# Loops written out on every engine after the first attention, and a constant moved from SBUF to a PSUM column

## The reference, cut to what matters

```
x = x + tanh(g_xattn[0]) * attention0(layernorm(x), ctx)            # 16 heads, softmax
x = x + tanh(g_ffn[0])   * bitnet(layernorm(x))                     # quantised 256->1024, conv of 3 taps, silu, quantised 1024->256
x = x + tanh(g_xattn[1]) * attention1(layernorm(x), ctx, Wq, Wk, Wv) # projections with relu, 16 heads
x = x + tanh(g_ffn[1])   * experts(layernorm(x))                    # 8 experts of width 128, the 2 best of 2 groups
```

## Time and profile before

| | us |
|---|---|
| median of 3 runs | 1893.88 |
| lowest and highest of them | 1891.81, 1896.88 |
| the profiled execution | 1889.21 |
| its span, first to last instruction | 1887.5 |

### The profile page before, as it was taken

The page is one execution under the profiler, slowest core; times in us unless marked ns, Lnnn a source line. Parts: engine busy times, 40 slices in busy tenths (PEclk is TensorE's granted clock), DMA queues, the critical chain, the costliest instruction groups (busy, mean ns, idle before and its releaser), DMA issues. The chain is left out here.

```text
span 1887.5 us, 52415 instructions
## 1 busy us (share of the span) xinstructions
PE 1598.1 (85%) x20058; PEld 1093.4 (58%) x20058; DVE 1574.0 (83%) x2977; ACT 1186.2 (63%) x1916; POOL 865.3 (46%) x932
## 2 busy tenths in 40 slices
PE   0799999846766676748999999996899999999998
PEld 0677777623444444435777777775465565655655
DVE  7799999858888889876888888886888888888885
ACT  1799989778777787716888888886233333323332
POOL 1455555427777777753333333332233333333332
PEclk9999999979999989969999999998899999999999
DMA  9200000000000000000002000000221211222212
GB/s 313 89 3 3 3 3 3 3 0 1 1 0 0 0 0 0 0 17 2 3 2 69 2 2 2 2 2 2 68 91 57 101 67 56 100 67 70 98 57 68
DMA packets 45470, 67.43 MB, mean 36 GB/s; under 512 B 6272, under 2 KB 36736, under 8 KB 45312
## 3 DMA queue, kind: packets, MB, share of 16 engines
q1 hardware_dynamic: 42944, 65.03, 10.4%
q10 hardware_dynamic: 2368, 0.02, 0.1%
HBM read 56.39 MB, written 8.65 MB: 34 GB/s over the span
## 5 line engine op out<-in xcount | busy, mean ns | idle before, releaser
L716 ACT ACTIVATE a_exp<-a_score_t 128x1024 f32<-128x1024 f32 x256 | 262.4, 1025 | 82.5 <-PE a_score_t L526 81.8
L641 DVE TENSOR_REDUCE a_maxes<-a_score 128x8 f32<-128x1024 f32 x256 | 311.0, 1215 | 0.5 <-PE a_score L509 0.5
L1539 POOL TENSOR_TENSOR e_a_parts<-e_act,e_a_parts 128x512 f16<-128x512 f32 x128 | 153.3, 1198 | 332.5 <-ACT e_a_parts L1510 332.5
L1510 ACT ACTIVATE e_a_parts<-e_act 128x512 f16<-128x512 f32 x128 | 80.6, 630 | 314.1 <-DVE e_act L1342 309.2
L1087 POOL TENSOR_TENSOR b_hidden<-b_hidden,b_shifted 128x508 f32<-128x508 f32 x128 | 161.7, 1263 | 124.4 <-DVE b_hidden L937 124.1
L1224 PE MATMUL e_up_ps<-e_n_turned,e_up_t 128*128 128x512 f16 x768 | 187.9, 381 | 9.7 <-DVE e_act L1338 9.7
L1238 PE MATMUL e_out<-e_down_t,e_a_parts 128*128 128x256 f16 x1536 | 188.5, 273 | 0.8 <-POOL e_a_parts L1539 0.8
L1224 PE MATMUL e_gate<-e_n_turned,e_gate_t 128*128 128x512 f16 x768 | 187.9, 381 | 0.2 <-issue 0.2
L1238 PEld LDWEIGHTS e_out<-e_down_t,e_a_parts 128*128 128x128 f16 x1536 | 149.6, 98 | 39.1 <-POOL e_a_parts L1539 1.1
L1094 POOL TENSOR_TENSOR b_hidden<-b_hidden,b_scales 128x512 f32<-128x512 f32 x128 | 168.2, 1318 | 2.9 <-ACT b_scales L1069 2.9
L774 POOL TENSOR_TENSOR a_split<-ctx,a_split 128x256 f16<-128x256 f16 (+1 forms) x64 | 42.9, 671 | 268.6 <-ACT a_split L733 268.6
(11 more groups left out here) (206 smaller groups left out, 4041.7 us busy)
## 6 DMA issues: line engine op xcount, KB each, us to landing
ctx<-e_weights SPq DMA_DIRECT2D x64, 512.0 KB, 5.7
out<-x SPq DMA_DIRECT2D x16, 512.0 KB, 2.9
x<-in_x SPq DMA_DIRECT2D x3, 2048.0 KB, 19.0
ctx<-in_ctx SPq DMA_DIRECT2D x1, 4096.0 KB, 27.0
ctx<-in_ctx SPq DMA_DIRECT2D x1, 3072.0 KB, 16.5
a_exp<-in_L_ffn_w SPq DMA_DIRECT2D x2, 1024.0 KB, 9.7
x<-in_x SPq DMA_DIRECT2D x1, 1536.0 KB, 16.4
ctx<-in_ctx SPq DMA_DIRECT2D x1, 1024.0 KB, 13.4
```

What stands on the lines that cost most here:

```text
L641: nc.vector.tensor_reduce(maxes[:, p * PAIRS:(p + 1) * PAIRS], score[:, :].rearrange("p (h k) -> p h k", k=P), AX.X, ALU.max).then_inc(max ...
L716: nc.scalar.activation(exp32[:, u % 2, 2 * p:2 * p + 2, :], score_t[:, :].rearrange("p (g n) -> p g n", g=2), ACT.Exp, scale=DH ** -0.5 / ...
L1539: nc.gpsimd.tensor_tensor(a_parts[:, e % 4, 1, :], act3[:, e % 2, :], a_parts[:, e % 4, 0, :], ALU.subtract).then_inc(alo_ok, 1)
```

## The change

`run_steps` becomes `write_steps` for VectorE, ScalarE and GpSimd in the second attention, for all four compute engines in the bitnet stage, and for these four and SyncE in the expert stage. The first attention keeps its loops. The SBUF column `level` is dropped; 1/127 goes to column 1 of the PSUM bank `magic`, and L962 and L973 read it there.

```
 # attention_stage, in each of VectorE, ScalarE, GpSimd
-                run_steps(dve, step, UNROLL, head, TILES, last_lag)
+                if layer:
+                    write_steps(step, UNROLL, TILES, last_lag)
+                else:
+                    run_steps(dve, step, UNROLL, head, TILES, last_lag)
...
 # bitnet_stage
-        level = sb("level", [P, 1])
...
-                run_steps(pe, step, 2, head, GROUPS, lag)
+                write_steps(step, 2, GROUPS, lag)
...
-                nc.vector.memset(level[:], 1.0 / 127.0).then_inc(level_ok, 1)
+                nc.vector.memset(magic[:, 1:2], 1.0 / 127.0).then_inc(level_ok, 1)
...
-                    nc.vector.scalar_tensor_tensor(out=peak_mid[:], in0=peak_mid[:], scalar=1e-5, in1=level[:, 0:1].broadcast_to([P, GT]),
+                    nc.vector.scalar_tensor_tensor(out=peak_mid[:], in0=peak_mid[:], scalar=1e-5, in1=magic[:, 1:2].broadcast_to([P, GT]),
...
-                    nc.vector.scalar_tensor_tensor(out=peak_in[:], in0=peak_in[:], scalar=1e-5, in1=level[:, 0:1].broadcast_to([P, GT]),
+                    nc.vector.scalar_tensor_tensor(out=peak_in[:], in0=peak_in[:], scalar=1e-5, in1=magic[:, 1:2].broadcast_to([P, GT]),
...
 # expert_stage, in each of SyncE, TensorE, VectorE, ScalarE, GpSimd
-                run_steps(pe, step, 2, head, GROUPS, lag, first=2)
+                write_steps(step, 2, GROUPS, lag, first=2)
```

More of the change, by code:

```diff
@@ L764, in step @@
                                              scale=gate[:, 0:1]).then_inc(v_ok, 1)
-                run_steps(act, step, UNROLL, head, TILES, last_lag)
+                if layer:
+                    write_steps(step, UNROLL, TILES, last_lag)
+                else:
+                    run_steps(act, step, UNROLL, head, TILES, last_lag)
             @block.gpsimd
@@ L796, in step @@
                         nc.gpsimd.tensor_tensor(m.x[:, t, :], m.x[:, t, :], mixed[:, (u - FL) % 2, :], ALU.add).then_inc(fin_ok, 1)
-                run_steps(pool, step, UNROLL, head, TILES, last_lag)
+                if layer:
+                    write_steps(step, UNROLL, TILES, last_lag)
+                else:
+                    run_steps(pool, step, UNROLL, head, TILES, last_lag)
 def bitnet_stage(nc, io, m):
@@ L1018, in step @@
                                                     x_turned[:, u % 2, d, 0, :, :], ALU.subtract).then_inc(lo_ok, 1)
-                run_steps(dve, step, 2, head, GROUPS, lag)
+                write_steps(step, 2, GROUPS, lag)
             @block.scalar
@@ L1074, in step @@
                                                  ACT.Copy).then_inc(hi_ok, 1)
-                run_steps(act, step, 2, head, GROUPS, lag)
+                write_steps(step, 2, GROUPS, lag)
             @block.gpsimd
@@ L1094, in step @@
                             nc.gpsimd.tensor_tensor(h, h, scales[:, (u - back) % 2, :], ALU.mult).then_inc(mult_ok, 1)
-                run_steps(pool, step, 2, head, GROUPS, lag)
+                write_steps(step, 2, GROUPS, lag)
 def load_experts(nc, sp, io, m):
@@ L1212, in step @@
                         spread_weights(s - 1, u - 1)
-                run_steps(sp, step, 2, head, GROUPS, lag, first=2)
+                write_steps(step, 2, GROUPS, lag, first=2)
                 sp.wait_ge(stored, 16 * GROUPS)
@@ L1463, in step @@
                             norm(s)
-                run_steps(dve, step, 2, head, GROUPS, lag, first=2)
+                write_steps(step, 2, GROUPS, lag, first=2)
             @block.scalar
@@ L1514, in step @@
                             split(s)
-                run_steps(act, step, 2, head, GROUPS, lag, first=2)
+                write_steps(step, 2, GROUPS, lag, first=2)
             @block.gpsimd
@@ L1542, in step @@
                             split_low(s)
-                run_steps(pool, step, 2, head, GROUPS, lag, first=2)
+                write_steps(step, 2, GROUPS, lag, first=2)
 def build_program(nc, io):
```

## The result

The changed kernel takes 1878.66 us in the median of 4 runs (1877.62 to 1879.04), beside 1894.95 us for the kernel before on the same chip. The ratio is 0.9915, with a 95% interval from 0.9898 to 0.9932: 16.1 us, 0.85% faster. The forecast was 1881.6 us, with a range from 1872 to 1891. The profiled execution took 1878.45 us, 10.8 less than that of before; its span is 1876.7 us. By the traces the 10.8 are 5.3 us in the bitnet stage, 4.4 in the experts and 1.2 in the first attention. The code of the first attention is unchanged, and over the runs that keep its loops its length varies by 2.3 us (310.0 to 312.3, from the first to the last L641), so the 1.2 is no part of the change.

A forecast was written before the change was run, and what follows sets the result against it. PE was taken to bound the second attention and nearly the experts, a multi-engine chain the bitnet stage. Terms 0 + 4.3 + 0 + 1.0 + 6.2 + 0.8 = 12.3 us gave a median of 1881.6 us, range 1872 to 1891.

The forecast's parts named there:

- What bounds the kernel: Per stage: PE in the second attention and nearly so in the experts; a chain through several engines in the bitnet stage.
- Second attention, SP's stream: Writing out the second attention's loops, and SP's stream in the experts, was costed at 0 us each.
- Experts: Expert stage loops written out: 0.36 us less in each of 12 steps, 4.3 us in all.
- a second, smaller hold: PE at the turning of the experts' routing weights: the rest of the 0.36 us a step beyond the up product.
- The constant: L962 in the bitnet stage no longer held by POOL: 0.48 us in 13 steps, 6.2 us, plus 0.8 at pipeline's end.
- The bitnet loops: Bitnet stage loops written out: 0.17 us for each pair of steps, 1.0 us in all.
- The sum against the profiled execution: Whole kernel: terms summing to 12.3 us, taken from the profiled 1889.2 us, give 1876.9 us.
- From there to the median: Whole kernel: the profiled execution lay 4.7 us below the median of 1893.88 us, so the median forecast was 1881.6 us.
- The constant's gain: Rival, bitnet chunk 3: waiting for ACT takes back what L962 wins, leaving 5.3 us from loops, 1888.6 us; chance 0.14.
- waited for instructions: Rival, written-out stages: engines stand still for 20 to 30 more instruction packets, about 20 us, 1902 us; chance 0.08.
- Returning: Rival, all loops: each return fetches its code again, so 21 us more are won, 1861 us; chance 0.04.
- The clock's drops: Rival, bitnet steps: without three slow steps 1876.5 us, chance 0.08; with four more slow steps 1888.4 us, chance 0.06.

The follow-up runs named there:

- the extra matmuls: PE repeats the coming chunk's product, unused, before both input turnings of each bitnet step; added to the changed kernel 1871.84 us, to the kernel before 1883.88 us.

## Why the prediction was right, point by point

**What bounds the kernel.** Right for each stage: the second attention gave nothing, the experts what PE could win, the bitnet stage what its chain could win. The parts measured alone are 0 + 4.0 + 6.0 + 6.1 = 16.1 us, and so is the whole; each part is uncertain by some 2 us, and the two edits of the bitnet stage share some of their gain, so the exact agreement is chance.

**Second attention, SP's stream.** Costed at 0; no change in the stage's 427.0 us, nor in the time.

**Experts.** Forecast 4.3, measured 4.0 us, and 4.5 in the stage of the profile. The step is the 34.10 us of the written one. What the prediction called a second, smaller hold, the turning of the routing weights, is the larger: 0.27 us of a step, against 0.11 at the up product.

**The constant.** The mechanism was right: the hold goes, the gain stops at ACT's tap, and DVE waits 0.51 us there. Forecast 6.2 + 0.8 = 7.0; measured 6.1 with the loops kept, and 5.6 after the loops, where a step gains 26.09 - 25.69 = 0.40 us and not 0.48, and the step in which the loop began gains nothing. The two edits of this stage share 0.09 us a step.

**The bitnet loops.** This term was mis-sized: "Written out I give each pair 0.17 us" took the shorter of the two steps for one without a loop's cost. It has 0.09 us of its own. The chain's part is 2.6 us by the stage once the clock's falls cost nothing: about 0.16 in each of 11 steps and 0.85 in the one that misses the hold. The times of the same two kernels say 3.4. The Trainium skill, "Advanced Engine Details and Errata", Control Flow Timing, whose branch gave an estimate of 0.65, is lower than all of these; by that figure, 0.11 of the 0.34 us that a pair gains would be the branch. What the remaining 2.6 to 3.4 of the 6.0 us are isn't shown: the 6.0 alone are uncertain by 2.3 us. The clock may have them: a slow step costs 1.46 to 1.70 us in that kernel and 1.46 to 1.79 in the kernel before, and their number differs between executions of one code. Counted by the starts of chunk 0, the three profiled executions with the bitnet code of before (that of before, of the second attention's loops alone and of the experts' loops alone) have 3, 6 and 5 slow steps; that of the bitnet loops alone has 4.

**The sum against the profiled execution.** The forecast was 1876.9, and the profiled execution of after took 1878.45. In the bitnet stage 8.0 us were forecast. The stage with the extra matmuls shows 404.1 - 395.9 = 8.2, the chain without the clock. In the two profiled executions it shows 409.0 - 403.7 = 5.3, since after has five slow steps and before only three. That 8.2 meets 8.0 is luck: the constant came out 1.4 us lower than forecast and the loops 1.6 higher. With the extra matmuls in both kernels, whole profiled executions differ by 1882.16 - 1870.41 = 11.75 us, against the 12.3 of the sum.

**From there to the median.** The step that subtracted 12.3 from the median of 1893.88 took the clock's bill to be the same in both kernels. Measured were 16.1 us, 12.9 at least by the interval, so 12.3 lies just under it. The profiled execution of before, with three slow steps, was 5.7 us under its median of 1894.95; that of after is 0.2 under its own. With extra matmuls in both kernels the ratios are 0.9961 and 0.9893: 0.0068 x 1891 = 12.9 us. The other 3 us would be the clock, which by these ratios costs before 7.4 us and after 4.2; by the medians after pays 6.8, by the stage in the profiles 7.8. The comparisons have an uncertainty of the same size, so how the last 3 us divide stays open.

**The rivals.** The constant's gain wasn't taken back. No engine waited for instructions: the Trainium skill, "Runtime: NRT & Kernel Launch", Instruction fetch mechanics, says that straight code is streamed with its cost mostly hidden, and 56 more packets without idle time agree. Returning wasn't dear either: all loops together gave 9.1 us, not the 21 and more of that rival. The clock's drops met the shorter steps elsewhere, at 20 us instead of mostly at 16 to 17; in the profiles they cost five steps 6.9 us, against 4.9 us for three before. Neither of the two forecasts for them came true.

## What to carry to other kernels

Look for a tiny instruction that lasts as long as its neighbour on GpSimd, and give it an operand in PSUM; count what that wins only up to the next wait on the same engine. Before writing a loop out, see which engine sets that stage's pace, and check afterwards whether an instruction now starts together with one on another engine that makes it longer: here that cost 22 us. Where a step's length jumps without a change in its work, look at the granted clock, at the place in the step where it falls, and at what waits for TensorE there.

## What the runs showed that was not expected

- A one-tensor `tensor_scalar` of 128x4 elements is held for 1.18 us by a GpSimd instruction, like the two-tensor form; with a PSUM column 0.16 us.
- With GpSimd's start at 0.01 instead of 0.11 us behind VectorE's, VectorE's 128x256 normalisation takes 0.84 instead of 0.40 us in the mean of the tiles, and the kernel is 22 us slower.
- Eight useless matmuls a step made the kernel 6.8 us faster by the medians (4.2 by the ratios, 7.8 in the profiles' bitnet stage). The granted clock still fell to the 1.2 GHz level, but at another place of the step, where the next step did not become late by it.
- Writing the loops out moved one of the held instructions out of its neighbour's way: in one step it took 0.25 instead of 1.18 us, and that step alone gained 0.84 us.
